# Attention scores in a fused transformer layer: full-height products or pairs of 64-row tiles

## What is computed

```python
qkv = x @ w_qkv + b_qkv                                  # x normalised
attn = einsum('bnd,bmd->bnm', q * scale, k)              # 1024 x 1024 for each head
rel_h = einsum('bhwc,hkc->bhwk', r_q, Rh)                # 32 values for each query: key row
rel_w = einsum('bhwc,wkc->bhwk', r_q, Rw)                # 32 values for each query: key column
attn = attn + rel_h[..., :, None] + rel_w[..., None, :]
out = softmax(attn) @ v
x = x + out @ w_proj + b_proj
x = x + moe(layernorm(x))                                # 8 experts, two for each token
```

## Time and profile before

| | us |
|---|---|
| median of 3 runs (lowest to highest) | 602.42 (601.74 to 602.75) |
| the profiled execution | 603.15 |
| its span, first to last instruction | 601.3 |
| TensorE busy / mean granted clock | 587.1 / 0.993 |
| VectorE busy | 383.0 |
| ScalarE busy | 295.2 |
| GpSimd busy | 196.7 |
| maxima, TensorE L584: 192 matmuls | 77.0 busy |
| scores, TensorE L597: 384 matmuls | 115.3 busy |
| exponents, ScalarE L979: 96 | 98.1 busy |
| reductions, VectorE L1188: 192 | 130.8 busy |
| sums, GpSimd L423: 58 | 139.7 busy |

### The profile page before, as it was taken

The page is one execution under the profiler, slowest core; times in us unless marked ns, Lnnn a source line. Parts: engine busy times, 40 slices in busy tenths (PEclk is TensorE's granted clock), DMA queues, the critical chain, the costliest instruction groups (busy, mean ns, idle before and its releaser), DMA issues.

```text
span 601.3 us, 11451 instructions
## 1 busy us (share of the span) xinstructions
PE 587.1 (98%) x4459; PEld 511.5 (85%) x4459; DVE 383.0 (64%) x643; ACT 295.2 (49%) x411; POOL 196.7 (33%) x115
## 2 busy tenths in 40 slices
PE   7999999999999999999989999999999999999996
PEld 7787977766677766668988999999999999999994
DVE  6646777777677776624888865554567555367525
ACT  4555245555555555563646444454545444455523
POOL 2300068889899888897000000000000000000000
PEclk9999999999999999999889999999999999999999
DMA  8046064444333334103412444443443434543202
GB/s 264 21 87 134 1 132 89 89 90 87 71 68 67 69 75 87 40 3 106 157 41 81 157 158 158 155 146 130 133 147 105 150 141 159 158 157 97 101 1 105
DMA packets 38615, 63.40 MB, mean 105 GB/s; under 512 B 3912, under 2 KB 34478, under 8 KB 38446
## 3 DMA queue, kind: packets, MB, share of 16 engines
q1 hardware_dynamic: 38574, 62.83, 37.0%
HBM read 44.16 MB, written 1.57 MB: 76 GB/s over the span
## 4 chain that ended last, share of the span: by engine, by line
PE 91%; DVE 3%; DMA 2%; ACT 1%; SPq 1%; issue 1%; DVEq 0%
PE ps L822 21%; PE ps L838 21%; PE ps L597 13%; PE ps L606 9%; PE ps L501 8%; PE ps L584 7%; PE ps L533 2%; PE ps L756 1%; PE ps L793 1%; PE ps L544 1%; PE ps L849 1%; PE ps L768 1%; SPq L336 1%; DMA kst<-kp 1%; PE ps L630 1%
## 5 line engine op out<-in xcount | busy, mean ns | idle before, releaser
L1188 DVE TENSOR_REDUCE rhalf<-ps 128x1 f32<-128x512 f32 x192 | 130.8, 690 | 33.6 <-PE ps L584 33.3
L423 POOL TENSOR_TENSOR acc<-acc,prob 128x1024 f32<-128x1024 f32 x58 | 139.7, 2408 | 8.7 <-ACT prob L979 4.0
L979 ACT ACTIVATE prob<-ps 128x1024 f32<-128x1024 f32 x96 | 98.1, 1028 | 80.7 <-PE ps L597 80.3
L597 PE MATMUL ps<-qst,kst 128*128 128x512 f32 x384 | 115.3, 396 | 0.5 <-DMA qst<-mneg 0.3
L451 POOL CAST dpc<-dpt 120x1024 fp32r<-120x1024 f32 (+1 forms) x3 | 3.1, 1042 | 274.8 <-PE ps L858 216.6
L822 PE MATMUL ps<-xeh,wih 128*128 128x320 f32 x288 | 89.6, 311 | 1.0 <-ACT xeh L1043 1.0
L838 PE MATMUL ps<-hh,woh 128*128 128x320 f32 x288 | 89.2, 310 | 0.0
L838 PE MATMUL ps<-hh,wol 128*128 128x320 f32 x288 | 89.0, 309 | 0.0
L822 PE MATMUL ps<-xeh,wil 128*128 128x320 f32 x288 | 89.0, 309 | 0.0
L838 PE MATMUL ps<-hl,woh 128*128 128x320 f32 x288 | 89.0, 309 | 0.0
L822 PE MATMUL ps<-xel,wih 128*128 128x320 f32 x288 | 89.0, 309 | 0.0
(11 more groups left out here) (162 smaller groups left out, 883.6 us busy)
## 6 DMA issues: line engine op xcount, KB each, us to landing
raw_i<-in_L_ffn_wi SPq DMA_DIRECT2D x32, 576.0 KB, 5.2
raw_o<-in_L_ffn_wo SPq DMA_DIRECT2D x32, 576.0 KB, 4.1
xs<-in_x SPq DMA_DIRECT2D x8, 384.0 KB, 4.7
qst<-qh SPq DMA_DIRECT2D x12, 256.0 KB, 3.1
qst<-relh SPq DMA_DIRECT2D x12, 256.0 KB, 3.9
qst<-relw SPq DMA_DIRECT2D x12, 256.0 KB, 4.4
kst<-kp SPq DMA_DIRECT2D x12, 256.0 KB, 5.1
qst<-ql SPq DMA_DIRECT2D x12, 128.0 KB, 3.0
```

The costliest lines, as they stand in the source:

```text
L423: nc.gpsimd.tensor_tensor(acc[:, :], acc[:, :], prob[:, slot_of(j, t), :], ALU.add).then_inc(sum_add, 1)
L597: last = mm(bank(2 * (t % 2) + half), kst[b][:, part, t * P:(t + 1) * P], qst[b][:, part, half * BANK:(half + 1) * BANK], start=part == 0, ...
L979: run(prob[:, slot_of(j, t), :], ps[:, 2 * (t % 2) * BANK:2 * (t % 2 + 1) * BANK], ACT.Exp).then_inc(exp_done, 1)
L1188: ve.tensor_reduce(rhalf[:, p // 2, p % 2:p % 2 + 1], bank(max_bank(b, p)), AX_X, ALU.max).then_inc(max_red, 1)
```

## The change

Scores and maxima use the lower and the upper 64 rows of the array as two tiles. `OWN` (rows 0 to 31 and 96 to 127) hold q and k of both halves, `NEAR` (rows 32 to 63 and 64 to 95) the bias terms. A side is one half of the queries, so `qm[b]` has four slots of 512 queries: LOW (q low, w terms low, and the negated maximum), HIGH (q high, w terms high), and two slots (q high again, with h terms high and low) for the first and the second half of the keys. `scores(h, b, t)` is three units (HIGH, slot 2 + t // 4, LOW) of two matmuls, one for each side, into two banks: 48 matmuls of 64 rows in 24 pairs. Only the third unit of tile 0 waits for the negated maximum. Maxima are 16 matmuls of 64 rows in 8 pairs (p, p + 1), both sides with the same keys.

The h terms are no longer in the maxima products: `reduce_max` reduces 512 columns to 16 values (one for each key row), and `whole_max` adds `relhn` (128 x 8 x 32) to all of them and reduces again. The w terms are shifted by a column of their own (`rcol`, `rel_shift`), which frees a row of the tile for the maximum.

The terms go through two DRAM tables (`near_w`, `near_h`), written by `near_rows(c)` for each of the three chunks of four heads and read by `gather_head`. `gather_head` has eight transfers, `max_row` two, and SP's order is changed. One tile more goes past GpSimd (ADDED 6 for 7). The loop over heads on VectorE is written out. `turn_attn` reads another layout.

```diff
-            gather_head(0)
-            gather_head(1)
+            near_rows(0)
+            gather_head(0)
+            near_rows(1)
+            near_rows(2)
+            gather_head(1)
+            max_row(0)
             for h in range(NH):
-                max_row(h)
                 if h + 2 < NH:
                     gather_head(h + 2)
+                if h + 1 < NH:
+                    max_row(h + 1)
...
+            def near_rows(c):
+                heads = slice(HPG * c, HPG * (c + 1))
+                sp.wait_ge(rel_act, 4 * (c + 1))
+                sp.wait_ge(rel_dve, 4 * (c + 1))
+                for side in range(2):
+                    cols = slice(side * BANK, (side + 1) * BANK)
+                    parts = [(near_w[heads, side, :, :, :], relw[:, c, side, :, :])]
+                    for part in range(2):
+                        parts.append((near_h[side, part, :, heads, :, :].rearrange("i h v n -> (h v) i n"), relh[:, part, c, cols]))
+                    for dst, src in parts:
+                        sp.dma_start(dst, src.bitcast(F32)).then_inc(near_out[c], 16)
...
             def max_row(h):
                 sp.wait_ge(mneg_ready, h + 1)
+                for half, row in enumerate(MAX_ROW):
+                    sp.dma_start(qm[h % 3][row:row + 1, LOW, :].rearrange("o (t q) -> o t q", q=P).bitcast(F32),
+                                 mneg[half * HALF:(half + 1) * HALF, :].bitcast(F32)).then_inc(mrow_in, 16)
...
+                for side, own in enumerate(OWN):
+                    cols = slice(side * BANK, (side + 1) * BANK)
+                    parts += [(km[b][own, :, :], kp[rows, :, chunk, :]),
+                              (qm[b][own, HIGH:4, :], qh[rows, chunk, cols].unsqueeze(1).broadcast_to([HD, 3, BANK])),
+                              (qm[b][own, LOW, :], ql[rows, chunk, cols])]
...
+                sp.wait_ge(near_out[chunk], 16 * NEAR_DMAS)
+                for slots, src in ((slice(0, 2), near_w[h, :, :, :, :]), (slice(2, 4), near_h[:, :, :, h, :, :])):
+                    sp.dma_start(qm[b][HD:3 * HD, slots, :].bitcast(F32), src).then_inc(heads_in[b], 16)
...
+            def scores(h, b, t):
+                wait(pe, exp_done, NT * h + t - 1)
+                units = [(HIGH, 0), (2 + t // HALF, 1), (LOW, 0)]
+                for k, (q_slot, k_slot) in enumerate(units):
+                    if k == 2 and t == 0:
+                        pe.wait_ge(mrow_in, 32 * (h + 1))
+                    for side in range(2):
+                        rows = slice(side * P // 2, (side + 1) * P // 2)
+                        last = mm(bank(2 * (t % 2) + side), km[b][rows, k_slot, t * P:(t + 1) * P],
+                                  qm[b][rows, q_slot, :], start=k == 0, stop=k == 2)
...
+                scores(h, b, 0)
+                if first:
+                    pe.wait_ge(v_dve, NT)
+                scores(h, b, 1)
+                next_max(3)
+                if not first:
+                    values(h - 1, (b - 1) % 3, 2)
+                    values(h - 1, (b - 1) % 3, 3)
...
+                next_max(4)
+                scores(h, b, 2)
+                next_max(5)
+                scores(h, b, 3)
+                if not first:
+                    turn_output(h - 1)
+                next_max(6)
+                scores(h, b, 4)
+                next_max(7)
+                scores(h, b, 5)
...
+                values(h, b, 0)
+                values(h, b, 1)
+                if not last:
+                    turn_max(h + 1, (b + 1) % 3)
+                after_max(0)
+                scores(h, b, 6)
+                after_max(1)
+                scores(h, b, 7)
+                after_max(2)
...
                 if t == HALF:
                     turn_max(0, 0)
+                    pe.wait_ge(rows_in[0], 16)
+                if t > HALF:
+                    for p in range(2 * (t - HALF - 1), 2 * (t - HALF)):
+                        max_scores(1, 0, 1, p)
...
+            def rel_shift(n):
+                kind, c, half = REL[n]
+                if kind == 1:
+                    dve.wait_ge(rel_col, 2 * c + half + 1)
+                    wait(dve, rel_mm, n - 3)
+                    ve.tensor_tensor(rst[:, half, :].rearrange("p (g k) -> p g k", k=SIDE),
+                                     bank(n % 2).rearrange("p (g k) -> p g k", k=SIDE),
+                                     rcol[:, half, :].unsqueeze(2).broadcast_to([P, P // 8, SIDE]),
+                                     ALU.subtract).then_inc(relw_shifted, 1)
...
             def whole_max(h):
                 dve.wait_ge(max_red, 2 * NT * (h + 1))
+                ve.tensor_tensor(rhalf[:, :, :], rhalf[:, :, :],
+                                 relhn[:, h // HPG, :, h % HPG * SIDE:(h % HPG + 1) * SIDE], ALU.add).then_inc(max_sum, 1)
+                dve.wait_ge(max_sum, h + 1)
                 ve.tensor_reduce(rmax[:, :], rhalf[:, :, :], AX_X, ALU.max).then_inc(max_whole, 1)
```

More of the change, by code:

```diff
@@ new lines, in next_max, with after_max @@
+                def next_max(k):
+                    if not last:
+                        for p in (2 * k, 2 * k + 1):
+                            max_scores(*nxt, p)
+                def after_max(k):
+                    if more and not last:
+                        if first and k == 0:
+                            pe.wait_ge(rows_in[1], 16)
+                        for p in (2 * k, 2 * k + 1):
+                            max_scores(*after, p)
+                scores(h, b, 0)
+                if first:
+                    pe.wait_ge(v_dve, NT)
```

250 lines of the change are left out of this document (118 added, 132 removed).

## The result

The changed kernel takes **641.58 us** (median of four runs, 638.42 to 642.02) against 602.08 us for the kernel before (601.74 to 602.75, four runs): a ratio of 1.0635, 95% interval 1.0609 to 1.0661. The forecast was 594.8, with 587 to 605 as its range. The profiled execution has a span of 640.4 us against 601.3.

The account below looks back on a forecast made before the run. TensorE was taken as the bound, busy 16.5 of 16.5 us a head. From 603.15 us profiled: first block +6.6, nine periods -12.8, tenth -1.3, last head +0.5, +1.2, -1.9; "together -7.9", median 594.5, stated 594.8, range 587 to 605.

Parts of the forecast that it names:

- 5.8 us at 365 GB/s: Before the heads: SP's write of each chunk's 2.1 MB table was priced at 5.8 us, at 365 GB/s.
- tables crowd out heads 1 and 2: Rival, SP's queue from 58 to 98 us: tables written at 200 GB/s take 10.5 us each; 605 us, chance 0.15.
- The period: Loop of heads: spacing of value blocks, forecast to fall by 1.42 us to 15.1 us.
- Value block 3.19: TensorE's value block: 8 more instructions, 56 in all, lengthen it from 2.73 to 3.19 us.
- A pair's slot 0.232: TensorE's scores and maxima: two 64-row matmuls overlap fully, so a pair takes 0.232 us.
- Reductions of 16 values: VectorE's maxima: reducing 512 columns to 16 values costs nothing more; spaced 0.61 us, at most 0.69.
- Changes of form: TensorE's switches of tile form: 0.09 us each, seven in a head, three of them on the loop.
- rival 2: TensorE: each of seven form changes drains the array, 0.39 us; period 16.4, time 606 us; chance 0.07.
- TensorE's own list 13.7: TensorE's work in a head: pairs 7.4, values 5.0, turns 0.6, changes 0.6; 13.7 us, idling 1.4.
- Block to turn 7.45: From value block to turn of the maxima: VectorE's reductions and h-term addition set 7.45 us, TensorE waiting 1.1.
- an addition over 0.6: Sign of being wrong: VectorE's addition of the h terms, priced at 0.42 us, taking over 0.6.
- Turn to block 4.45: Turn of the maxima to next value block: 3.2 us to tile 0's LOW unit, then 1.25 us.

Follow-up runs that it names:

- e1: Changed kernel with the DRAM tables laid out so each write has 128 rows as slowest dimension, reads split to match; 610.32 us, ratio 1.0124.
- e3: Changed kernel without DRAM tables: bias rows copied tile to tile, sixteen transfers a head; 606.05 us, ratio 1.0062 to the kernel before.
- e14: e3 with the six transfers that a maximum product reads issued first, under a semaphore of their own; 605.50 us, ratio 1.0045.
- e7: e3 with maximum pair M4 moved inside the value block and M5 ahead of the scores of tile 2; 610.95 us, ratio 1.0142.
- e16: e10 with the transfers that maximum products read issued first, and GpSimd's additions whole in the last head; 594.64 us, ratio 0.9869.
- e10: e5 with each of GpSimd's additions cut into four of 256 columns; 600.41 us, ratio 0.9964.
- e4: Changed kernel with GpSimd's additions after the first cut to 8 columns, so its output is not the layer's; 634.17 us, ratio 1.0541.
- e8: e5 and e7 together; 606.86 us, ratio 1.0087 to the kernel before.
- e5: e3 with the h terms' addition and the last reduction made in three parts, behind reductions 7, 11 and 15; 628.38 us, ratio 1.0437.
- e15: e5 with GpSimd's additions cut into two of 512 columns; 606.35 us, ratio 1.0065.

## Why the prediction was wrong

**The tables: the step that failed.** "5.8 us at 365 GB/s" took the rate of a well spread transfer, the output's stores, for one whose slowest dimension is 4 or 8. The writes ran at 71 to 127 GB/s, and the first table took from 32.69 to 55.16 us, 22.5 us for 5.8. Head 1's first maximum tile was forecast at 82 and started at 113.71, head 0's block at 102.0 and started at 136.03: 31.7 of the 34.0 us are there when head 1's rows have come. The mechanism was among the rivals (tables crowd out heads 1 and 2, 0.15), and its place, SP's queue from 58 to 98 us, was right (the second and third table were issued from 69.1 to 95.5); but I bounded the rate below at 200 GB/s, a gather's, and so the time above at 605. The shape of a transfer gives its rate, and I had looked only at bytes and at row length. With the layout of e1 my 365 held (344 to 397 GB/s), and the block started at 104.62, 2.6 us from the forecast. That is the forecast's table term shown right by the edit that makes its assumption true.

**What I left out altogether** was the clock: TensorE idle fell to 0.50, and the v tiles behind the stall took 3.18 us for 1.56. A stall of TensorE ahead of dense work cost more than its length here, in e3 and in e14 as well.

**The period.** Forecast 15.1, measured 16.37, over ten heads 12.7 us. By terms:
- Value block 3.19: measured 3.16. A pair's slot 0.232: three pairs in 0.70. Right.
- Reductions of 16 values: 0.683 mean, spaced 0.61. Right.
- Changes of form: the block around M4 in e7 grew by 0.57 for a 0.23 slot and two changes, at most 0.17 each where I had 0.09. Small, and rival 2 (0.39 each) is out.
- TensorE's own list 13.7: it takes 15.5. This term was wrong by more than the addition's. Score tiles (5.7), values (5.1) and turns (0.8) are near what I had; the eight maximum pairs take 3.76 us in e16's chain where I had 1.86 and 0.6 for all changes of form. In four of the eight the second side waits for its bank, that is for one of VectorE's reductions, and the score tile behind it starts late; my sum of TensorE's work had no such wait. In e10 and e16, where the additions no longer hold it up, the period is 15.48 and 15.47, still over the 15.1 forecast.
- Block to turn 7.45: measured 8.22 (188.44 to 196.66). The addition was priced at 0.42 like an instruction that reads one operand from PSUM, and took 1.10. This is 0.68 of the 0.77 missing. I had given "an addition over 0.6" as a sign of being wrong, without asking what could make it so. e4 and e10 measure the leg without it: from mark to turn 8.20 and 7.94 us for 8.84.
- Turn to block 4.45: measured 4.98 (196.66 to 201.64), and the same from turn to mark (7.53) in every run that leaves the value block as it is. VectorE's first reduction starts 0.74 behind the turn where I had 0.54, and S0 with S1 takes 1.58 to 1.65 for twelve matmuls, 1.39 as six slots. The maximum's row, on which I had this leg end, held nobody back in the loop.

**The rest.** GpSimd's 12.3 us stay hidden as forecast, but GpSimd wasn't free of consequence: it was read as cover and not as a neighbour on the same operand path. The last head and the tail were within 0.5 us.

**Slips of arithmetic.** The terms of the sum give -7.7, not -7.9. Its nine periods run from 95.44, not from 111.96. And rival 2 by its own terms is 607.8, not 606. All three are small against the miss.

So the sum of -7.9 contained two wrong terms: +6.6 for the start (it was +40.6) and about -14.1 for the periods (it was -1.5). e16, which mends both causes and keeps the pairs, comes to 594.64, near the 594.8 forecast; that is luck and not the prediction come true, as its period (15.47) is longer and its start (97.69) earlier than in my sum, and it has edits that the change lacks.

## What to carry to other kernels

Price a transfer by its shape: read the DMA share of a transfer with the same slowest dimension, and where there is none, take a share of 4 or 8 sixteenths as a bound; one dimension merged into another was worth 31 us here. Beside a busy GpSimd a VectorE operation with two SBUF operands costs what is left of GpSimd's instruction and 0.08 to 0.28 us more, so keep it off the path, don't split it alone, and shorten the instructions on the other side. And a cut of a third in one engine's work gives what the loop through the other engines lets through: close that loop term by term, count the waits inside the engine's own list too, and for each short operation ask who else is running.

## What the runs showed of the hardware

- Two matmuls on 64-row tiles, each side with a bank of its own, start 1 to 4 ns apart when neither waits; three pairs of 512 columns take 0.70 us, as long as three single 128-row matmuls. A maximum pair whose second side waited for its bank started 0.245 us apart.
- A VectorE addition of two SBUF operands takes 0.22 us for 64 columns and 0.29 for 128 alone, and up to 2.25 (e8) and 2.29 (e5) beside GpSimd additions of 2.41; the longest of either falls to 1.24 beside instructions of 1.28 (e15) and to 0.78 and 0.86 beside those of 0.745 (e10, e16).
- An addition of VectorE that had to wait ended 0.08 us (64 columns), 0.15 (128) or 0.28 (256) behind the end of GpSimd's instruction.
- GpSimd's addition took 2.41 us for 1024 columns, 1.28 for 512 and 0.745 for 256. A tile of 1024 columns took 2.46, 2.59 and 2.91 us from start to start in one, two and four pieces: some 0.13 to 0.15 us for each further piece.
- The same table bytes moved at 71 to 127 GB/s with 4 or 8 as slowest dimension (6.8 packets in flight on average) and at 344 to 397 with 128 (16.1).
- TensorE's granted clock was 0.50 from 89 to 119 us, in its idle time and in the v tiles behind it, 3.18 us for nine matmuls instead of 1.56. Behind a wait of 3.3 us (e14) a value block took 4.85 us instead of 3.16.
